# Projection pieces halved over more token turns, and two score rows placed ahead of the last turn, in a one-layer language model tower

## The chip, the cores and the metric

The kernel runs on one core of one Trainium2 chip. The metric is the device time of one execution in microseconds (us), the median of the runs. The engines are TensorE (PE: matmuls and transposes), VectorE (DVE), ScalarE (ACT), GpSimd (POOL) and SyncE (SP, here the issuer of most DMAs). They share memory and run their own instruction queues in order, tied together by semaphores.

## What is computed

2048 tokens (2 sequences of 1024) go through an embedding, one attention layer and one mixture-of-experts layer. In short:

```
is_hot  = hot_mask[tok]; hot_vec = hot_emb[tok2hot[tok]]; cold_vec = cold_emb[tok2cold[tok]] @ proj_w.T
h       = where(is_hot, hot_vec, cold_vec)                     # [2048, 512]
q, k, v = layernorm(h) @ w_project.T    (16 heads of 32)
h       = h + softmax(causal(q k^T / sqrt(32))) v @ w_out.T
h       = h + shared_ffn(layernorm(h)) + top-2 of 16 experts   # routed by layernorm(h) @ Wr.T + bias
```

tok2hot and tok2cold are counted out from the list of the 8000 hot ids in the kernel itself.

## The kernel before, in words

**Stages.** First a table over the vocabulary is built (64 pairs of one-hot products on PE). Then comes the token stage, on which the change acts, from about 35 us to 109 us of the span; then attention in 8 units (4 groups of heads by 2 sequences), the output projection, the router and the experts.

**Token stage.** The tokens are 16 tiles of 128 (NT = 16). A *look* (L1959 to L1967) is three bf16 matmuls that fetch a tile's table rows into one PSUM bank; a *lookup* (look_up, L1865) is the two reductions of DVE that read that bank. EARLY_LOOKS looks and lookups run ahead of the loop, the others inside it. row_numbers (L1877) turns the lookups of a group of tiles (ROWS_TO gives the group ends) into row numbers, and POOL gathers the cold and the hot rows of a tile with two indirect DMAs (L1764, L1768), tile by tile, with inv_std (L887) of an earlier tile behind each pair.

PE's loop runs over turns c = 0 to 18 (L1972). Turn c, in this order: transpose the cold rows of tile c (L1978), when its gather has landed; project tile c-1 (L1988), which needs ACT's copy of the transposed cold rows (L1805); transpose the normalized tile c-3 (L1996); look(EARLY_LOOKS + c - 1), while there are looks left; and a *piece* of unit 0's first projections if c is in FIRST_FILL (first_piece, L613). DVE's loop, iteration c: first_low for a piece (L594), embed(c) (L1890: L1895 adds the projected cold vector to the hot one, L1897 to L1899 are the statistics), norm(c-1) (L1901), a part of the weights' split (L537), look_up(EARLY_LOOKS + c - 1) and, at the end of a group, row_numbers. embed(c) needs the projection that PE issues in turn c+1. ACT's loop: copy of the cold transpose, copy of xnT for tile c-3 (L1809), first_high (L580).

**PSUM.** There are 8 banks. Before: cold transposes in banks 0 and 6 in turns, projections in 1 and 5, xn transposes in 2 and 3, looks in 4 and 5 (tiles 0 to 10) or 4 and 7 (tiles 11 to 15), pieces in 7. A look waits until the lookup two tiles back is done:

```
def look_bank(c):
    return bank(4 if c % 2 == 0 else 5 if c < EARLY_LOOKS else 7)
...
if c >= 2:
    pe.wait_ge(s_looked, 2 * (c - 1))
```

**First pieces.** FIRST_FILL = {7: 0, 8: 1, 10: 4, 12: 2, 14: 3, 16: 5} gives for a turn the piece: 0 and 1 are q and k for the first 512 tokens, 2 and 3 q and k for the next 512, 4 and 5 the values. A piece of q or k is 4 fp32 matmuls (8 records) of 512 columns; ACT writes its high part (first_high), DVE its low part (first_low), and both read the piece's bank.

**SP's queue.** It is in order (L1684): the store of tile c's h (L1686) when embed(c) is done; behind the store of tile 7 the 16 DMAs that stack q of the first half into q_stack and behind that of tile 8 the 16 for k_low (stack_half, L439 to L453), when the low part of the piece is ready; behind the store of tile 15 the 16 for the other half of q_stack and 16 for k_high. ACT and DVE begin attention when all 16 stores have landed.

**Attention.** A unit has 32 score rows of 128 queries (8 query tiles by 4 heads). Rows 0 to 15 need k_low and the first half of q_stack only; row 16 (NARROW) is the first that needs k_high (L690). Unit 0 begins with first_scores (L745), rows 0 and 1; row n+2 is issued in step n.

Of the kernel before, what the change touches and what calls it, by code (L numbers as in the profile page):

```python
# [11 lines left out]
F32 = mybir.dt.float32  # L12
# [8 lines left out]
P = 128  # L21
# [21 lines left out]
EARLY_LOOKS = 11  # L43
FIRST_FILL = {7: 0, 8: 1, 10: 4, 12: 2, 14: 3, 16: 5}
# [25 lines left out]
def build(nc, a, out):  # L70
    ctx = ExitStack()
    with ctx:
# [319 lines left out]
        ROWS_TO = [0, 2, 6, 11, NT]  # L392
# [81 lines left out]
        def look_bank(c):  # L474
            return bank(4 if c % 2 == 0 else 5 if c < EARLY_LOOKS else 7)

# [103 lines left out]
        def first_high(act, c):  # L580
# [6 lines left out]
            if side == 0:  # L587
                act.activation(part_hi[:, 0, cols], bank(7), ACT.Copy, scale=-ATT_SCALE).then_inc(s_hi, 1)
            elif side == 1:
                act.copy(part_hi[:, 1, cols], bank(7)).then_inc(s_hi, 1)  # L590
            elif half == 0:
                act.copy(v_unit[0][:, 0:4, :].rearrange("p a n -> p (a n)"), bank(7)).then_inc(s_fact, 1)

        def first_low(dve, c):  # L594
# [5 lines left out]
            if side < 2:  # L600
                dve.wait_ge(s_hi, HEAD + 2 * half + side + 1)
                if side == 0:
                    dve.scalar_tensor_tensor(out=part_lo[:, 0, cols], in0=bank(7), scalar=-ATT_SCALE,
                                             in1=part_hi[:, 0, cols].bitcast(F32), op0=ALU.mult,
                                             op1=ALU.subtract).then_inc(s_lo, 1)
                else:
                    dve.tensor_tensor(part_lo[:, 1, cols], bank(7), part_hi[:, 1, cols].bitcast(F32),
                                      ALU.subtract).then_inc(s_lo, 1)
            elif half == 1:
                dve.wait_ge(s_fill, HEAD + n + 1)  # L610
                dve.tensor_copy(v_unit[0][:, 4:8, :].rearrange("p a n -> p (a n)"), bank(7)).then_inc(s_fdve, 1)

        def first_piece(pe, c):  # L613

            f = FIRST_FILL[c]
            pe.wait_ge(s_wq if f < 4 else s_w, 16)
            pe.wait_ge(s_xC, 4 if f in (0, 1, 4) else 8)
            if f == 0:
                pe.wait_ge(s_looked, 2 * NT)
            elif f == 2:  # L620
                pe.wait_ge(s_fact, HEAD + 3)
            else:
                pe.wait_ge(s_lo, HEAD + {1: 1, 4: 2, 3: 3, 5: 4}[f])
            for k in range(KC):
                if f < 4:
                    side, half = f % 2, f // 2
                    mm = pe.matmul(bank(7), w_unit[:, k, side * P:(side + 1) * P],  # L627
                                   xnT[:, k, half * 512:half * 512 + 512],
                                   start=(k == 0), stop=(k == KC - 1), skip_group_check=True)
                else:  # L630
                    mm = value_products(pe, 0, f, k)
            mm.then_inc(s_fill, 1)

        def fill_piece(pe, u, b, f, k, loads):
# [17 lines left out]
            else:  # L652
                mm = value_products(pe, b, f, k)
# [3 lines left out]
        def value_products(pe, b, f, k):  # L657

            t0 = b * SEQ + ((f - 4) * 4 + k) * P
            for c in range(KC):  # L660
                mm = pe.matmul(bank(7)[:, k * P:(k + 1) * P], xnT[:, c, t0:t0 + P],  # L661
                               w_unit[:, c, 2 * P:3 * P], start=(c == 0), stop=(c == KC - 1))
            return mm

# [9 lines left out]
        def att_pe(pe):  # L674
# [78 lines left out]
            first_scores(0, 0, 0)  # L753
# [1301 lines left out]
```

## Time and profile before

| what | value |
|---|---|
| median of 3 runs | 965.74 us (964.69 to 966.0) |
| the profiled execution's own time | 964.48 us |
| its span in the trace | 962.7 us |
| PE busy | 899.1 us (93%) |
| DVE, ACT, POOL busy | 658.3, 604.0, 439.7 us |
| chain that ended last: PE, SP's queue, DVE, "issue" | 73%, 8%, 7%, 5% |

The busy times are sums over the whole span. The chain that ended last is followed back from the last instruction; a share of SP's queue in it means stretches in which the order and the pace of DMA issues set the end. The change touches only the stretch from about 35 to 128 us, so timelines of that stretch are what is to be read.

### The profile page before, as it was taken

How to read it: one execution, taken by the hardware profiler on the slowest of the kernel's cores; microseconds unless marked ns; L12 is line 12 of the kernel's file. 1: busy time of each engine (PE TensorE's matmuls, PEld its weight loads, DVE VectorE, ACT ScalarE, POOL GpSimd, SP SyncE). 2: the span in 40 equal slices, each digit the busy share in tenths (PEclk: the TensorE clock that was granted, in tenths of full speed). 3: DMA queues.
4: the chain of work that ended last, by engine and by line, in shares of the span. 5: the costliest groups of instructions: out<-in, count | busy, mean ns of one | idle time of the engine just before them, and what ended most of it. 6: DMA issues, size and time to landing. Idle time of an engine off the chain costs nothing.

```text
span 962.7 us, 21706 instructions
## 1 busy us (share of the span) xinstructions
PE 899.1 (93%) x6859; PEld 684.3 (71%) x6859; DVE 658.3 (68%) x1657; ACT 604.0 (63%) x1318; POOL 439.7 (46%) x486
## 2 busy tenths in 40 slices
PE   6778899999999999999997899999999999999995
PEld 5335678787887978878785677767776776776673
DVE  8886567576666757666675767868877666666662
ACT  6323577776777777777787833331157777777773
POOL 9276553533515346251500415633344577356332
PEclk9799999999999999999999999999999999999998
DMA  6135442324324242332313521271459478736530
GB/s 232 42 101 139 131 115 57 97 57 102 98 56 100 49 118 68 81 97 52 98 44 92 216 89 77 80 282 55 177 177 388 146 138 188 258 61 129 61 44 1
DMA packets 60514, 110.53 MB, mean 115 GB/s; under 512 B 15412, under 2 KB 21556, under 8 KB 58098
## 3 DMA queue, kind: packets, MB, share of 16 engines
q1 hardware_dynamic: 48082, 87.15, 29.1%
q0 software_dynamic: 12320, 21.99, 12.0%
q8 instruction: 57, 0.93, 0.4%
q14 instruction: 55, 0.45, 0.2%
HBM read 53.03 MB, written 25.17 MB: 81 GB/s over the span
## 4 chain that ended last, share of the span: by engine, by line
PE 73%; SPq 8%; DVE 7%; issue 5%; ACT 2%; POOL 2%; DMA 1%; ACTq 0%; POOLq 0%; DVEq 0%
PE psum L1576 13%; PE psum L705 10%; SPq L451 8%; PE psum L1654 8%; PE psum L718 6%; PE psum L695 6%; PE psum L661 5%; PE psum L648 5%; PE psum L670 5%; PE psum L1495 3%; PE psum L1608 2%; PE psum L1598 2%; PE psum L627 1%; PE psum L1587 1%; PE psum L721 1%
## 5 line engine op out<-in xcount | busy, mean ns | idle before, releaser
L792 ACT ACTIVATE probs<-psum,nmax 128x128 f32<-128x128 f32 (+7 forms) x256 | 191.2, 747 | 37.1 <-DVE nmax L834 33.7
L834 DVE CUSTOM_DVE_ANT_0 psum<-psum,mask_row 128x128 f32<-128x128 f32 (+7 forms) x256 | 192.1, 766 | 26.6 <-PE psum L695 25.1
L705 PE MATMUL psum<-ident,probs 128*128 128x128 f32 x1152 | 174.6, 276 | 13.0 <-ACT probs L792 6.1
L705 PEld LDWEIGHTS psum<-ident,probs 128*128 128x128 f32 x1152 | 134.1, 140 | 48.6 <-ACT probs L792 18.3
L777 ACT COPY probsT<-psum 128x512 f32<-128x512 f32 (+3 forms) x256 | 129.2, 505 | 33.2 <-PE psum L705 30.5
L1068 POOL DMA_INDIRECT out<-xnT,slot_out x47 | 81.4, 1732 | 100.8 <-DMA out<-xnT,slot_out 68.5
L488 POOL CAST part_hi<-full 128x512 fp32r<-128x512 f32 x28 | 17.1, 610 | 206.1 <-ACT full L565 160.3
L695 PE MATMUL psum<-k_low,q_stack 128*128 128x512 f32 (+2 forms) x256 | 104.3, 415 | 6.2 <-ACT probs L792 2.6
L849 DVE TENSOR_TENSOR attnT<-psum,z_rows 128x128 f32<-128x128 f32 x64 | 18.6, 291 | 111.3 <-ACT z_rows L799 111.3
L1654 PE MATMUL psum<-w_dn,gated_T 128*128 x188 | 88.4, 593 | 1.0 <-ACT gated_T L1131 1.0
L1418 DVE TENSOR_TENSOR w_lo<-w_gu,w_hi 128x1024 fp32r<-128x1024 f32 x48 | 58.7, 1225 | 40.4 <-ACT w_hi L1160 39.4
L1418 DVE TENSOR_TENSOR ws_lo<-w_gu,ws_hi 128x1024 fp32r<-128x1024 f32 x46 | 56.3, 1226 | 37.5 <-ACT ws_hi L1160 36.7
L718 PE MATMUL psum<-probsT,v_unit 128*32 128x128 f32 x2304 | 76.2, 275 | 0.0
L515 POOL TENSOR_TENSOR x_lo<-xnT,x_hi 128x512 fp32r<-128x512 f32 x56 | 71.8, 1282 | 4.4
L718 PEld LDWEIGHTS psum<-probsT,v_unit 128*32 128x32 f32 x2304 | 59.0, 109 | 15.5 <-ACT probsT L777 7.8
L661 PE MATMUL psum<-w_unit,xnT 128*128 128x128 f32 x512 | 66.6, 275 | 0.0
L779 DVE COPY probsT<-psum 128x128 f32<-128x128 f32 (+3 forms) x128 | 62.2, 486 | 3.9 <-PE psum L705 2.9
L695 PEld LDWEIGHTS psum<-k_low,q_stack 128*128 128x128 f32 x256 | 51.2, 203 | 15.0 <-ACT probs L792 10.9
L661 PEld LDWEIGHTS psum<-w_unit,xnT 128*128 128x128 f32 x512 | 61.7, 192 | 0.0
L1145 ACT ACTIVATE xnT<-psum,slot_w 128x512 f32<-128x512 f32 x47 | 32.4, 689 | 41.7 <-PE psum L1654 41.7
L1160 ACT CAST w_hi<-w_gu 128x1024 fp32r x48 | 50.3, 1050 | 8.9 <-issue 5.6
L1654 PEld LDWEIGHTS psum<-w_dn,gated_T 128*128 128x128 f32 x188 | 35.5, 189 | 27.6 <-issue 23.7
(280 smaller groups left out, 2134.2 us busy)
## 6 DMA issues: line engine op xcount, KB each, us to landing
w_gu<-in_wgu SPq DMA_DIRECT2D x16, 1024.0 KB, 6.7
q_stack<-part_hi SPq DMA_DIRECT2D x128, 64.0 KB, 2.0
q_stack<-part_lo SPq DMA_DIRECT2D x128, 64.0 KB, 2.0
w_dn<-in_wd SPq DMA_DIRECT2D x16, 512.0 KB, 8.6
out<-acc SPq DMA_DIRECT2D x17, 256.0 KB, 3.6
hot_all<-xn SPq DMA_DIRECT2D x4, 1024.0 KB, 8.6
h_scratch<-hot_all SPq DMA_DIRECT2D x16, 256.0 KB
k_low<-part_hi SPq DMA_DIRECT2D x64, 64.0 KB, 2.0
```

The lines of the kernel that those rows point to most:

```text
L451: sp.dma_start(dst.bitcast(F32), src[32 * h:32 * h + 32, side, half * 512:half * 512 + 512].bitcast(F32)).then_inc((s_high if half else s_ ...
L661: mm = pe.matmul(bank(7)[:, k * P:(k + 1) * P], xnT[:, c, t0:t0 + P], w_unit[:, c, 2 * P:3 * P], start=(c == 0), stop=(c == KC - 1))
L695: mm = pe.matmul(dst[:, c0:c1], qs, ks[:, h, 0:c1 - c0], start=True, stop=True)
L705: mm = pe.transpose(bank(4 + m % 2)[:, (j - 4 * k) * P:(j - 4 * k + 1) * P], probs[n % PSLOTS][:, j * P:(j + 1) * P], ident[:, :])
L718: pe.matmul(bank(6)[32 * h:32 * h + 32, 0:P], v_unit[b][:, j, 32 * h:32 * h + 32], probsT[i % 2][:, h, j * P:(j + 1) * P], start=(j == 0), ...
L777: eng.copy(dst, src).then_inc(s_Ca, 1)
L792: act.activation(probs[n % PSLOTS][:, 0:(i + 1) * P], score_bank(n)[:, 0:(i + 1) * P], ACT.Exp, bias=nmax[:, n % 4:n % 4 + 1], scale=-1.0, ...
L834: dve.tensor_tensor_reduce(out=row, in0=row, in1=mask_row[:, (QT - 1 - i) * P:QT * P], scale=1.0, scalar=3.0e38, op0=ALU.add, op1=ALU.min, ...
L1068: pool.indirect_dma_start(out=out, out_offset=bass.IndirectOffsetOnAxis(ap=slot_out[:, j:j + 1], axis=0), in_=y_rows[j % ROUTED_RING], in_ ...
L1418: dve.tensor_tensor(w_lo[j % 2][:, k, :].rearrange("p k n -> p (k n)"), w_gu[:, bass.ds(slot, 1), k, :].rearrange("p o k n -> p (o k n)"), ...
L1576: mm = pe.matmul(bank(2 + p), x[:, p, k * P:(k + 1) * P], w[p][:, k, :], start=(k == 0 and t == 0), stop=(k == KC - 1 and t == 2), skip_gr ...
L1654: mm = pe.matmul(bank(6 + p), gated_T[:, p, k * P:(k + 1) * P], w_dn[:, bass.ds(half, 1), k, :].rearrange("p o n -> p (o n)"), start=(k == 0),
```

## The change

- The first pieces are halved: each half (2 of the 4 k-steps) goes into one of the turns 6 to 17 (FIRST_TURN = 6), the second half in the turn that FIRST_FILL names. Pieces use banks 7 and 6 in turns.
- The cold transposes move into two parts of bank 0, and each waits for the copy of the one before.
- Looks: eight run ahead of the loop (EARLY_LOOKS = 8). From tile 8 on all use bank 4, and each waits for the lookup of the tile before.
- The row numbers come in five groups, ending at tiles 2, 6, 10, 13 and 16.
- DVE's first_low stands behind norm in its iteration.
- The first two score rows of unit 0 (scores_ahead) are issued in turn 17, ahead of the transposes of tile 15 in turn 18. What first_scores waited for is waited for at attention's start.

```diff
-EARLY_LOOKS = 11
-FIRST_FILL = {7: 0, 8: 1, 10: 4, 12: 2, 14: 3, 16: 5}
+EARLY_LOOKS = 8
+FIRST_FILL = {7: 0, 9: 1, 11: 4, 13: 2, 15: 3, 17: 5}
+FIRST_TURN = 6
...
-        ROWS_TO = [0, 2, 6, 11, NT]
+        ROWS_TO = [0, 2, 6, 10, 13, NT]
...
         def look_bank(c):
-            return bank(4 if c % 2 == 0 else 5 if c < EARLY_LOOKS else 7)
+            return bank(5 if c % 2 and c < EARLY_LOOKS else 4)
+
+        def first_bank(f):
+            return bank(7 - list(FIRST_FILL.values()).index(f) % 2)
...
-            f = FIRST_FILL[c]
-            pe.wait_ge(s_wq if f < 4 else s_w, 16)
-            pe.wait_ge(s_xC, 4 if f in (0, 1, 4) else 8)
-            if f == 0:
-                pe.wait_ge(s_looked, 2 * NT)
-            elif f == 2:
-                pe.wait_ge(s_fact, HEAD + 3)
-            else:
-                pe.wait_ge(s_lo, HEAD + {1: 1, 4: 2, 3: 3, 5: 4}[f])
-            for k in range(KC):
+            half_piece = (c - FIRST_TURN) % 2
+            f = FIRST_FILL[c + 1 - half_piece]
+            if half_piece == 0:
+                pe.wait_ge(s_wq if f < 4 else s_w, 16)
+                pe.wait_ge(s_xC, 4 if f in (0, 1, 4) else 8)
+                if f == 3:
+                    pe.wait_ge(s_fact, HEAD + 3)
+                elif f in (4, 2, 5):
+                    pe.wait_ge(s_lo, HEAD + {4: 1, 2: 2, 5: 3}[f])
+                elif f == 1:
+                    pe.wait_ge(s_coldC, c)
+            for k in range(2 * half_piece, 2 * half_piece + 2):
...
-            mm.then_inc(s_fill, 1)
+            if half_piece:
+                mm.then_inc(s_fill, 1)
...
+        def scores_ahead(pe):
+
+            pe.wait_ge(s_low[0], STACKED)
+            pe.wait_ge(s_coldC, NT)
+            pe.wait_ge(s_h, NT - 1)
+            for h in range(2):
+                pe.matmul(bank(h)[:, 0:256], q_stack[:, h, 0:P], k_low[0][:, h, 0:256], start=True,
+                          stop=True).then_inc(s_S, 1)
...
-            first_scores(0, 0, 0)
+            pe.wait_ge(s_fact, HEAD + 3)
+            pe.wait_ge(s_fdve, HEAD + 3)
             unit(0, 0, 0, False, True)
...
-                    act.copy(cold_T[:, c % 2, :], bank(6 if c % 2 else 0)[:, 0:P]).then_inc(s_coldC, 1)
+                    act.copy(cold_T[:, c % 2, :], bank(0)[:, c % 2 * P:c % 2 * P + P]).then_inc(s_coldC, 1)
...
             for c in range(NT + 1):
-                if c in FIRST_FILL and c < NT:
-                    first_low(dve, c)
                 if c < NT:
                     embed(c)
                 if c >= 1:
                     norm(c - 1)
+                if c in FIRST_FILL:
+                    first_low(dve, c)
...
-            first_low(dve, NT)
+            first_low(dve, NT + 1)
...
             def look(c):
                 if c >= 2:
-                    pe.wait_ge(s_looked, 2 * (c - 1))
+                    pe.wait_ge(s_looked, 2 * (c if c >= EARLY_LOOKS else c - 1))
...
-                    if c >= 2:
-                        pe.wait_ge(s_coldC, c - 1)
-                    pe.transpose(bank(6 if c % 2 else 0)[:, 0:P], cold_lat[c][:, :],
+                    if c >= 1:
+                        pe.wait_ge(s_coldC, c)
+                    pe.transpose(bank(0)[:, c % 2 * P:c % 2 * P + P], cold_lat[c][:, :],
                                  ident[:, :]).then_inc(s_coldT, 1)
...
-                if c in FIRST_FILL:
+                if FIRST_TURN <= c < FIRST_TURN + 2 * FILLS:
                     first_piece(pe, c)
+                if c == NT + 1:
+                    scores_ahead(pe)
             pe.wait_ge(s_xC, NT)
+            pe.wait_ge(s_lo, HEAD + 4)
             att_pe(pe)
```

## Rows read from the trace of the kernel before

**Rows 1.** Chain of work, 36 to 130 us: start us, us, what

```profile
62.34 3.81 DMA cold_all<-in_cold_emb,cold_row
...
103.69 0.32 SPq L1686
...
125.61 2.03 DMA k_high<-part_lo
```

**Rows 2.** Timeline of PE, 88 to 128 us: start us, us, instructions, [idle before, releaser]

```profile
88.20 3.60 PE L627 MATMUL psum<-xnT,w_unit 128*128 128x512 f32 x8
91.64 0.27 PE L1978 MATMUL psum<-ident,cold_all 128*128 128x128 f32 x1
91.75 1.02 PE L1988 MATMUL psum<-projT,cold_T 128*128 128x512 f32 x2
92.61 0.60 PE L1996 MATMUL psum<-ident,xn 128*128 128x128 f32 x4
...
95.42 0.66 PE L1996 MATMUL psum<-ident,xn 128*128 128x128 f32 x4 [1.24 <-DVE xn L1906]
...
109.00 0.74 PE L695 MATMUL psum<-k_low,q_stack 128*128 128x256 f32 x4 [0.78 <-ACT xnT L1809]
...
127.78 0.47 PE L695 MATMUL psum<-k_low,q_stack 128*128 128x512 f32 x1 [0.42 <-DMA k_high<-part_lo]
```

**Rows 3.** Timeline of SP's queue, 73 to 107 us

```profile
73.69 2.53 SPq L451 DMA_DIRECT2D q_stack<-part_hi  x4
...
94.56 9.45 SPq L1686 DMA_DIRECT2D h_scratch<-hot_all  x7
104.05 2.41 SPq L451 DMA_DIRECT2D q_stack<-part_hi  x4
```

**Rows 4.** Timeline of DVE, 50 to 103 us

```profile
50.02 0.69 DVE L1895 TENSOR_TENSOR hot_all<-hot_all,psum 128x512 f32<-128x512 f32 x1 [0.42 <-PE psum L1988]
...
52.30 0.69 DVE L1895 TENSOR_TENSOR hot_all<-hot_all,psum 128x512 f32<-128x512 f32 x1 [0.45 <-PE psum L1988]
...
55.29 0.68 DVE L1895 TENSOR_TENSOR hot_all<-hot_all,psum 128x512 f32<-128x512 f32 x1
...
58.28 0.08 DVE L1873 DVE_READ_ACCUMULATOR prod<-iota_bf,tok_lo,psum 128x1 f32 x1
58.28 0.68 DVE L1895 TENSOR_TENSOR hot_all<-hot_all,psum 128x512 f32<-128x512 f32 x1
...
77.78 0.68 DVE L1895 TENSOR_TENSOR hot_all<-hot_all,psum 128x512 f32<-128x512 f32 x1
...
92.47 0.69 DVE L603 SCALAR_TENSOR_TENSOR part_lo<-psum,part_hi 128x512 fp32r<-128x512 f32 x1 [1.94 <-ACT part_hi L588]
...
102.98 0.68 DVE L1895 TENSOR_TENSOR hot_all<-hot_all,psum 128x512 f32<-128x512 f32 x1
```

**Rows 5.** Timeline of PE, 47 to 60 us

```profile
47.91 2.07 PE L1988 MATMUL psum<-projT,cold_T 128*128 128x512 f32 x2
...
52.09 0.38 PE L1964 MATMUL psum<-tab_a,tok_ohT 125*128 125x512 bf16 x1
...
52.59 1.02 PE L1988 MATMUL psum<-projT,cold_T 128*128 128x512 f32 x2
...
59.84 0.33 PE L1978 MATMUL psum<-ident,cold_all 128*128 128x128 f32 x1 [0.93 <-DMA cold_all<-in_cold_emb,cold_row]
```

**Rows 6.** Timeline of POOL: the gather of tile 2's cold rows

```profile
45.40 1.00 POOL L1764 DMA_INDIRECT cold_all<-in_cold_emb,cold_row  x1 [0.30 <-issue]
```

**Rows 7.** Stretches of 2 us: length, busy us of PE, PEld, DVE, ACT, POOL, PEclk, DMA share, GB/s

```profile
34.00:36.00 2.00, 0.97 (x4) 0.46 (x5) 0.94 (x6) 0.00 (x0) 0.00 (x0) 0.67 1.02 336
...
50.00:52.00 2.00, 2.00 (x6) 0.95 (x5) 1.72 (x4) 0.27 (x1) 0.37 (x2) 0.57 0.36 106
...
58.00:60.00 2.00, 0.98 (x7) 0.45 (x6) 1.90 (x6) 0.59 (x1) 1.80 (x3) 1.00 0.40 67
```

More of the change, by code:

```diff
@@ L587, in first_high @@
             if side == 0:
-                act.activation(part_hi[:, 0, cols], bank(7), ACT.Copy, scale=-ATT_SCALE).then_inc(s_hi, 1)
+                act.activation(part_hi[:, 0, cols], first_bank(f), ACT.Copy, scale=-ATT_SCALE).then_inc(s_hi, 1)
             elif side == 1:
-                act.copy(part_hi[:, 1, cols], bank(7)).then_inc(s_hi, 1)
+                act.copy(part_hi[:, 1, cols], first_bank(f)).then_inc(s_hi, 1)
             elif half == 0:
-                act.copy(v_unit[0][:, 0:4, :].rearrange("p a n -> p (a n)"), bank(7)).then_inc(s_fact, 1)
+                act.copy(v_unit[0][:, 0:4, :].rearrange("p a n -> p (a n)"), first_bank(f)).then_inc(s_fact, 1)
         def first_low(dve, c):
@@ L602, in first_low @@
                 if side == 0:
-                    dve.scalar_tensor_tensor(out=part_lo[:, 0, cols], in0=bank(7), scalar=-ATT_SCALE,
+                    dve.scalar_tensor_tensor(out=part_lo[:, 0, cols], in0=first_bank(f), scalar=-ATT_SCALE,
                                              in1=part_hi[:, 0, cols].bitcast(F32), op0=ALU.mult,
@@ L606, in first_low @@
                 else:
-                    dve.tensor_tensor(part_lo[:, 1, cols], bank(7), part_hi[:, 1, cols].bitcast(F32),
+                    dve.tensor_tensor(part_lo[:, 1, cols], first_bank(f), part_hi[:, 1, cols].bitcast(F32),
                                       ALU.subtract).then_inc(s_lo, 1)
@@ L610, in first_low @@
                 dve.wait_ge(s_fill, HEAD + n + 1)
[L611 removed]
+                dve.tensor_copy(v_unit[0][:, 4:8, :].rearrange("p a n -> p (a n)"), first_bank(f)).then_inc(s_fdve, 1)
         def first_piece(pe, c):
[L615 to L624 removed]
+            half_piece = (c - FIRST_TURN) % 2
[10 more added lines that the diff above has]
+            for k in range(2 * half_piece, 2 * half_piece + 2):
                 if f < 4:
                     side, half = f % 2, f // 2
[L627 removed]
+                    mm = pe.matmul(first_bank(f), w_unit[:, k, side * P:(side + 1) * P],
                                    xnT[:, k, half * 512:half * 512 + 512],
@@ L652, in fill_piece, with value_products @@
             else:
-                mm = value_products(pe, b, f, k)
+                mm = value_products(pe, b, f, k, bank(7))
             if k == KC - 1:
                 mm.then_inc(s_fill, 1)
-        def value_products(pe, b, f, k):
+        def value_products(pe, b, f, k, dst):
             t0 = b * SEQ + ((f - 4) * 4 + k) * P
             for c in range(KC):
-                mm = pe.matmul(bank(7)[:, k * P:(k + 1) * P], xnT[:, c, t0:t0 + P],
+                mm = pe.matmul(dst[:, k * P:(k + 1) * P], xnT[:, c, t0:t0 + P],
                                w_unit[:, c, 2 * P:3 * P], start=(c == 0), stop=(c == KC - 1))
             return mm
+        def scores_ahead(pe):
[5 more added lines that the diff above has]
+                          stop=True).then_inc(s_S, 1)
         def output_tile(pe, c):
```

2 lines of the change are left out of this document (1 added, 1 removed).

## The prediction

> **What bounds the kernel now.** I read the page first (PE is busy 93% of the span, so a stretch in which PE waits is worth looking for), then the chain of work over the stretch that the change touches, then the timelines of the engines on it, last POOL and the clock. "Tile c" is a tile of 128 tokens, "turn c" PE's turn c, "iteration c" DVE's; embed(c) is the L1895 addition.
>
> The chain runs back from score row 16 of unit 0, the first that needs the high halves of the keys: it starts at 127.78 after a wait of 0.42 us for k_high, whose last copy lands at 127.64 (125.61 + 2.03) [rows 1, 2]. Those copies stand in SP's queue: 32 stacking DMAs from 104.05, and just ahead of them the store of tile 15 at 103.69, which waits for embed(15) at 102.98 [rows 1, 3, 4]. Attention's first product starts at 109.00, but it ends at this same gate. So the end of the kernel moves with embed(15), as long as PE reaches row 16 in time; it took 18.8 us from 109.00 to 127.78.
>
> What sets embed(15)? In the piece turns PE works 3.43 us on a piece (88.20 to 91.64), DVE can't start embed until its low part has come out of that piece, and PE then idles 1.24 us for the norm (95.42) [rows 2]. Two turns take 7.7 us. Before that, in turns 4 to 7, PE waits for the gather of the cold rows (0.93 us at 59.84) [rows 5], and DVE is just as full: embed to embed 2.99 us (55.29 to 58.28) with a lookup in each iteration [rows 4].
>
> **The change, part by part.**
>
> Halved pieces and banks 6 and 7 in turns. The products are the same 6 pieces; 12 halves of 1.73 us (3.45 / 2). A turn without a piece costs PE 0.11 + 0.86 + 0.44 = 1.41 us (91.64, 91.75, 92.61, and 0.44 to the next transpose) [rows 2], with a half piece 3.14. The low part moves behind norm on DVE and the next half goes to another bank, so the idle 1.24 per pair should go: turns 9 to 16 run at 3.14 each instead of a mean of 3.60 (embed(8) at 77.78 to embed(15) at 102.98, seven turns, 25.2 us) [rows 4]. Gain in these seven: 25.2 - 22.0 = 3.2 us. I give back 0.5 for iteration 8, where DVE has lookup 15 and a group of row numbers to do and norm(8) comes late for turn 11.
>
> Eight looks ahead of the loop instead of eleven. Three looks and one group of row numbers leave the stretch before turn 0. But tile 2's cold rows are issued only at 45.40, and a gather lands 3.8 us after (62.34 + 3.81) [rows 1, 6]: 49.2. Turn 2 waits for it, and its projection takes 2.11 us at the clock of then (47.91 to embed at 50.02) [rows 4, 5], so embed(1) comes at about 51.8, against 52.30. Gain: 0.5.
>
> The looks left over. This is the term that decides. From tile 8 on all looks use bank 4, and look(c) waits for 2c reductions: for lookup(c-1). In turn t PE issues the projection of tile t-1, then look(t+7), and that waits for lookup(t+6). DVE does lookup(t+6) in iteration t-1, behind embed(t-1), which needs the projection that PE has just issued in the same turn; embed(t) needs the projection of turn t+1, queued on PE behind the look. So no part of DVE's iteration lies beside PE's turn any more. Before, the wait was for a look two back, with banks 4 and 7, and hid. The new period is: embed's start to lookup's end 3.07 (55.29 to 58.28 + 0.08) [rows 4]; handover 0.05 (47.91 + 2.07 to 50.02 shows 0.04) [rows 4, 5]; look and transpose 0.50 (52.09 to 52.59); projection 1.02 and handover 0.04 [rows 5]. Sum 4.68 us a turn, against 3.1 before. It holds for looks 9 to 15, turns 2 to 8. In turns 6, 7 and 8 the half piece stands behind the look, also in line: 4.68 + 1.73 = 6.41; in iteration 7 DVE has the first low part, 0.69 (92.47), between norm and lookup [rows 4].
>
> Clock. The periods above are at the granted clock 1.00. It was 1.00, then fell to half near 34.7 (a mean of 0.67 in 34 to 36), where PE was busy less than half of the time, and rose again within 50 to 52 (mean 0.57), in which PE is busy throughout [rows 7]. In the new kernel PE is busy from about 46.9 to 51.7 (projection 0, look 8, projection 1), as it was before the rise; I take it that the clock rises there again. The other end is that it stays at 1.2 GHz: then look and transpose cost twice 0.50 and the projection 2.11, 6.23 a turn, 1.55 more.
>
> The Trainium skill, "TensorE: Matmul & The Clock Gate", Part 1 (The HAM clock gate), says of this that "the default state is throttled, and activity releases the throttle": with PE idle for some 2.7 us of every 4.7, it speaks against this change, and by it the sum could be the one with the 1.55 in each turn. The trace agrees so far as it shows the fall after idleness and the rise after work.
>
> Gathers. The row numbers now come in iterations 2, 5 and 8. The last group is ready about 95, the gather of tile 13 lands near 99, and turn 13 is at about 103; covered by 4 us. If that cover went, each us late would be a us.
>
> Cold transposes share bank 0 and wait for the copy of the tile before; PE waited for that same copy one instruction later, so nothing. The wait of the first half piece for xnT of tile 3: about 0.7 us beside the look's stall of turn 6 (look(13) is later than that copy), nothing. ACT: same work, at other turns; nothing behind it is waited for.
>
> Scores ahead. Two products of row 0 move ahead of the last turn and could save at most the 0.78 of waiting at 109.00 [rows 2]. Row 16 waits for k_high anyway, so I count 0; at least one such wait stands ahead of it. At the other end, had SP time to spare, it would be worth 0.8.
>
> SP. Its queue is passed in order. The first q_stack copies wait for low part 0 (73.69 before), then 20.9 us of stacking and a store (73.69 to 94.56) stand ahead of tiles 9 to 15's stores [rows 3]. Now low part 0 comes after norm in iteration 7: 83.3, 2.2 (an iteration of 2.99 without its lookup) and 0.7 make 86.2, low part 1 in iteration 9, about 97.5, k_low's stack (half of the 20.9) ends near 108, six stores of 0.63 (2.53 / 4) end at 112. embed(15) is later than that, by a little.
>
> **Sum.** embed(1) 51.8; turns 3 to 6 bring embed(2) to embed(5), 4 x 4.68 = 18.7: 70.5; embed(6) and embed(7) 2 x 6.41 = 12.8: 83.3; embed(8) 6.41 + 0.69 = 7.1: 90.4 (before 77.78: 12.6 later). Then 22.0 + 0.5: embed(15) at 112.9, before 102.98. So +9.9 us. SP starts the high stacks that much later, k_high lands 23.6 later as before, near 137.5. PE, 18.8 us from attention's start (109.0 + 9.9), is there at the same time. Everything behind is shifted. Profiled execution: 964.48 (span 962.7) + 9.9 = 974.4; the median of the runs, 965.74, is 1.26 above it, so the forecast is 965.74 + 9.9 = 975.6. One measurement of this kernel can't tell under 0.2% (1.9 us) from nothing.
>
> **Rivals.**
>
> *The clock stays low* until the half pieces of turn 6: four turns at +1.55, 6.2 us more, 981.8. For: PE idles over half of each of these turns. Against: before, in 58 to 60, PE was busy for 0.98 of 2 us and the clock stayed at 1.00 [rows 7]. The Trainium skill's rule above is this case. Chance 0.28.
>
> *Faster.* The place is look(t+7) in turns 2 to 8. If lookup(t+6) were over when PE gets there, that is, if DVE ran one tile ahead of PE's projection, the stall wouldn't exist and only the better part would be left. Then low part 0 comes about 75.2 (behind embed and norm of its iteration instead of ahead of them, so 1.5 later than where its copies start now, 73.69), SP is through 20.9 us of stacking and seven stores of 0.63 at about 100.7 instead of 104.05: -3.3, 962.4. It decides at zero slack between the end of lookup and PE's arrival; by the order of both queues there is none. Chance 0.09.
>
> *Half paid.* The look is late in only some turns, for example because DVE's iteration gets shorter by itself: 2 to 6 us slower, 968 to 972. Chance 0.08. *Nothing to be seen*, gain and loss cancel: 0.03.
>
> **How the numbers follow.** Forecast 0.52. Slower: 0.52 + 0.28 + 0.08 = 0.88; faster 0.09; same 0.03. The range takes the forecast with its uncertain ends (1.26 of which execution, 0.5 of DVE, SP's close finish) and the low clock, with 1 us over: 970 to 983. Left out are the faster case, the same and part of the half paid one.
>
> **What would show it.** PE idle before L1964 for DVE prod, some 2.4 us in each of turns 2 to 8; embeds 4.7 apart, then 6.4, and 3.1 from tile 9 on; embed(15) near 113, k_high near 137.5 and row 16 right behind it. The granted clock from 52 to 75 tells the rival. Wrong it is if L1964 waits under 1 us, or if row 16 no longer waits for k_high.

## The result and the profile after

| what | before | after |
|---|---|---|
| median of 4 runs of each on one chip | 965.87 us (964.69 to 968.79) | 982.84 us (979.93 to 984.92) |
| ratio to before | | 1.0169 (95%: 1.013 to 1.0208) |
| the profiled execution's own time | 964.48 us | 984.63 us |
| its span | 962.7 us | 982.8 us |
| mean granted clock of PE over the span | 0.988 | 0.971 |
| embed(1), embed(8), embed(15) start at | 52.30, 77.78, 102.98 | 50.95, 99.93, 122.78 |
| first k_high row (row 16) starts at | 127.78 | 147.09 |

The changed kernel is 17.0 us slower, where 9.9 were forecast; the median is just inside the range (970 to 983), but not by the case that was taken as likeliest, and two of its four executions (984.63 and 984.92) lie outside. The executions lie 5 us apart, and they go with the mean granted clock: 979.93 us at 0.978, 981.05 at 0.976, the two longest at 0.971 and 0.973. The profiled one is near the upper end. It is 20.15 us over the profiled execution of before; all reckoning below is between these two, so what it gives for the clock is the price in one of the longer executions.

Line numbers have moved: embed is L1912 (L1895 before), the lookup L1890, the look L1981 to L1983 (L1964), the cold transpose L1995, the projection L2005, the transpose of xn L2013, a piece L633, the scores ahead L678, score rows L711, SP's stores L1703.

**Which wait grew.** The waits of PE between 44 and 126 us in the changed kernel (engine and line, what it waited for: us in total, times, longest us):

```profile
PE psum L1981 <- DVE prod L1890: 19.0, 7, 3.4
PE psum L1995 <- DMA cold_all<-in_cold_emb,cold_row: 1.9, 1, 1.9
PE psum L2013 <- DVE xn L1923: 0.7, 2, 0.5
```

and the same view of the kernel before, between 44 and 110 us:

```profile
PE psum L1996 <- DVE xn L1906: 5.8, 5, 1.3
PE psum L1978 <- DMA cold_all<-in_cold_emb,cold_row: 4.3, 4, 1.7
PE psum L1964 <- DVE prod L1873: 1.6, 2, 1.3
```

The waits for the norm (5.8 us) and for gathers (4.3 us) shrink, as the change means them to. The wait of the look for DVE's lookup goes from 1.6 us to 19.0 us, in seven times, the seven looks 9 to 15.

**The embeds.** The stage goes by them. The timeline of DVE in the changed kernel (start us, us, instruction, [idle before, releaser]) at embed(1), (2), (5), (6), (8) and (15):

```profile
50.95 0.69 DVE L1912 TENSOR_TENSOR hot_all<-hot_all,psum 128x512 f32<-128x512 f32 x1 [1.01 <-PE psum L2005]
...
56.97 0.69 DVE L1912 TENSOR_TENSOR hot_all<-hot_all,psum 128x512 f32<-128x512 f32 x1 [2.95 <-PE psum L2005]
...
74.90 0.69 DVE L1912 TENSOR_TENSOR hot_all<-hot_all,psum 128x512 f32<-128x512 f32 x1 [2.77 <-PE psum L2005]
...
83.08 0.69 DVE L1912 TENSOR_TENSOR hot_all<-hot_all,psum 128x512 f32<-128x512 f32 x1 [3.64 <-PE psum L2005]
...
99.93 0.69 DVE L1912 TENSOR_TENSOR hot_all<-hot_all,psum 128x512 f32<-128x512 f32 x1 [5.09 <-PE psum L2005]
...
122.78 0.69 DVE L1912 TENSOR_TENSOR hot_all<-hot_all,psum 128x512 f32<-128x512 f32 x1 [0.72 <-PE psum L2005]
```

From embed(1) to embed(5) they are 6.02, 6.02, 6.04 and 5.87 us apart, then 8.18, 8.07 and 8.78, where 4.68, 6.41, 6.41 and 7.10 were forecast. From embed(8) to embed(15) it is 22.85 us: 3.26 a turn, 25.20 before [rows 4]. So the sum against before is -1.35 (embed(1) at 50.95, not 52.30), +23.5 from there to embed(8) (48.98 us, not 25.48), and -2.35 for the last seven: +19.8.

**One stalled turn.** The timeline of PE in the changed kernel shows a whole period, from one look to the next, and the work just before it:

```profile
49.00 1.92 PE L2005 MATMUL psum<-projT,cold_T 128*128 128x512 f32 x2
54.09 0.61 PE L1981 MATMUL psum<-tab_a,tok_ohT 125*128 125x512 bf16 x1 [3.17 <-DVE prod L1890]
...
55.02 1.91 PE L2005 MATMUL psum<-projT,cold_T 128*128 128x512 f32 x2
56.73 1.06 PE L2013 MATMUL psum<-ident,xn 128*128 128x128 f32 x4
60.11 0.61 PE L1981 MATMUL psum<-tab_a,tok_ohT 125*128 125x512 bf16 x1 [2.32 <-DVE prod L1890]
```

The projection at 55.02 ends at 56.93, embed starts at 56.97, the lookup that follows it on DVE ends at 60.05 (59.97 + 0.08, beside the 3.07 us of the prediction), and the look starts at 60.11. Nothing lies beside anything: 2.84 us of PE, 0.04, 3.08 us of DVE, 0.06. That is the serial turn of the prediction. But look and transpose take 0.93 us (54.09 to 55.02), not 0.50, and the projection 1.91, not 1.02.

**The clock.** Stretches of 2 us of the changed kernel (length, busy us of PE, PEld, DVE, ACT, POOL, then the granted clock, share of the DMA engines, GB/s):

```profile
50.00:52.00 2.00, 0.92 (x2) 0.00 (x0) 1.01 (x2) 0.00 (x0) 1.80 (x3) 0.50 0.49 159
...
54.00:56.00 2.00, 1.92 (x6) 1.06 (x7) 0.03 (x2) 0.27 (x1) 1.56 (x2) 0.50 0.14 21
...
58.00:60.00 2.00, 0.00 (x0) 0.00 (x0) 1.93 (x8) 0.41 (x1) 0.79 (x1) 0.50 0.35 131
...
70.00:72.00 2.00, 0.00 (x0) 0.00 (x0) 1.93 (x7) 0.12 (x1) 0.88 (x2) 1.00 0.35 131
72.00:74.00 2.00, 1.81 (x6) 1.12 (x7) 0.13 (x2) 0.27 (x1) 1.70 (x2) 0.60 0.15 17
```

Before, the mean over 50 to 52 was 0.57, with PE busy throughout, and it was 1.00 afterwards [rows 7]. Here PE works only for the first 0.92 us of that stretch and then stands for 3.17 us. The clock stays at half of its rate (1.2 GHz) until about 69. After that it is badly timed as well as low: it is at 2.4 GHz in 70 to 72, in which PE does nothing, and 0.60 in the next stretch, in which PE works; the same again in 84 to 86 (1.00, PE idle) and 86 to 88 (0.51, PE busy 1.76 us). Not every working stretch is so slow: 78 to 80 has 0.81 and 82 to 84 has 0.84. The slices of the page that show the token stage (the granted clock in tenths, 40 slices of the span) say the same more coarsely, `57` here for `99` before in the third and fourth slice:

```profile
PEclk9757999999999999999999999999999999999998
```

**The end of the stage.** The timeline of SP's queue in the changed kernel:

```profile
94.08 2.53 SPq L452 DMA_DIRECT2D q_stack<-part_hi  x4
...
118.54 5.27 SPq L1703 DMA_DIRECT2D h_scratch<-hot_all  x7
123.86 2.42 SPq L452 DMA_DIRECT2D q_stack<-part_hi  x4
```

and the timeline of PE around attention's start and at row 16:

```profile
127.33 0.48 PE L678 MATMUL psum<-k_low,q_stack 128*128 128x256 f32 x2
...
128.98 0.50 PE L711 MATMUL psum<-k_low,q_stack 128*128 128x256 f32 x2 [0.73 <-ACT xnT L1826]
...
147.09 0.47 PE L711 MATMUL psum<-k_low,q_stack 128*128 128x512 f32 x1 [0.86 <-DMA k_high<-part_lo]
```

The seven stores of tiles 9 to 15 take 5.27 us here, 9.45 before [rows 3]: SP comes close to being late, but the last store still waits for embed(15) at 122.78. The last stacks (the second half of q_stack, then k_high) start 19.8 us later than before, k_high's last copy lands at 146.95 (144.92 + 2.03 in the chain of work), and row 16 starts right behind it, 19.3 us later. From row 16 to the end of the span it is 835.7 us (982.8 - 147.09), 834.9 before.

### The profile page after: what moved, and what is told of

It is laid out like the page before. It is cut to its first block, busy times and chain, and to the rows that moved or that the text cites. A ratio compares the mean times of both kernels' runs of the same rounds, so it can differ in the third digit from the quotient of the medians.

```text
span 982.8 us, 21715 instructions
## 1 busy us (share of the span) xinstructions
PE 910.7 (93%) x6859; PEld 689.8 (70%) x6859; DVE 659.3 (67%) x1664; ACT 604.4 (61%) x1318; POOL 439.9 (45%) x486
## 4 chain that ended last, share of the span: by engine, by line
PE 76%; DVE 9%; SPq 6%; issue 4%; ACT 2%; DMA 1%; POOL 0%; ACTq 0%; DVEq 0%; POOLq 0%
PE psum L1593 13%; PE psum L721 11%; PE psum L1671 8%; PE psum L734 6%; SPq L452 6%; PE psum L711 6%; PE psum L655 6%; PE psum L668 5%; PE psum L686 4%; PE psum L1512 3%; PE psum L1625 2%; PE psum L2005 2%; PE psum L1615 2%; PE psum L633 2%; PE psum L737 1%
## 5 line engine op out<-in xcount | busy, mean ns | idle before, releaser
L851 DVE CUSTOM_DVE_ANT_0 psum<-psum,mask_row 128x128 f32<-128x128 f32 (+7 forms) x256 | 192.0, 766 | 24.8 <-PE psum L711 23.6
L1085 POOL DMA_INDIRECT out<-xnT,slot_out x47 | 79.1, 1682 | 102.2 <-DMA out<-xnT,slot_out 65.0
L711 PE MATMUL psum<-k_low,q_stack 128*128 128x512 f32 (+2 forms) x254 | 104.0, 416 | 5.8 <-ACT probs L809 2.6
L711 PEld LDWEIGHTS psum<-k_low,q_stack 128*128 128x128 f32 x254 | 50.9, 203 | 14.5 <-ACT probs L809 9.9
```

The lines of the kernel that those rows point to most:

```text
L711: mm = pe.matmul(dst[:, c0:c1], qs, ks[:, h, 0:c1 - c0], start=True, stop=True)
L851: dve.tensor_tensor_reduce(out=row, in0=row, in1=mask_row[:, (QT - 1 - i) * P:QT * P], scale=1.0, scalar=3.0e38, op0=ALU.add, op1=ALU.min, ...
L1085: pool.indirect_dma_start(out=out, out_offset=bass.IndirectOffsetOnAxis(ap=slot_out[:, j:j + 1], axis=0), in_=y_rows[j % ROUTED_RING], in_ ...
```

## The experiments

The theory: the look that waits for the lookup just before it makes the turn serial, and with the clock, which the stall itself keeps low, that is the whole loss. The rivals: the loss comes from elsewhere in the change (the halved pieces, cold transposes in one bank, the scores ahead), or from the single bank as such. The kernel before was run anew with each set: 964.53 us (first set), 965.29 (second), 966.03 (third).

**The change without its looks.** Eleven early looks, two banks for the looks and the old wait come back; everything else of the change stays. The pieces go to banks 6 and 7 from the other end, so that bank 7 is free when the first one comes.

```diff
-EARLY_LOOKS = 8
+EARLY_LOOKS = 11
-        ROWS_TO = [0, 2, 6, 10, 13, NT]
+        ROWS_TO = [0, 2, 6, 11, NT]
...
-            return bank(5 if c % 2 and c < EARLY_LOOKS else 4)
+            return bank(4 if c % 2 == 0 else 5 if c < EARLY_LOOKS else 7)
...
-            return bank(7 - list(FIRST_FILL.values()).index(f) % 2)
+            return bank(6 + list(FIRST_FILL.values()).index(f) % 2)
...
-                    pe.wait_ge(s_coldC, c)
+                    pe.wait_ge(s_looked, 2 * NT)
...
-                    pe.wait_ge(s_looked, 2 * (c if c >= EARLY_LOOKS else c - 1))
+                    pe.wait_ge(s_looked, 2 * (c - 1))
```

> The changed kernel with the looks put back: eleven ahead of the loop, the other five in turns 1 to 5 in banks 4 and 7 in turns, each waiting for the lookup two back; the row number groups of before; piece halves, scores ahead and all else as changed, the pieces in banks 6 and 7 with piece 0 in bank 6. Theory (the wait for the lookup just before is the whole loss): no idle of over 1 us before a look in the loop; embeds 3.1 apart from tile 8 on; embed(15) near 97 instead of 102.98 before and 122.8 changed; k_high lands near 123.6, bound now by SP's queue from about 75 on; some 4 us faster than the kernel before, about 962. PE waits 2 to 3 us for k_high at row 16. Rival (the halved pieces or the shared cold bank cost too): embed(15) above 103 and the time above that of the kernel before.

Measured: 961.4 us (960.01 to 964.04, 10 runs), a ratio of 0.9971 (0.996 to 0.9981). It is 0.3% faster than the kernel before, and 21.4 us faster than the changed kernel's 982.84 (of another set). PE's waits between 44 and 128 us:

```profile
PE psum L711 <- DMA k_high<-part_lo: 2.6, 1, 2.6
...
PE psum L1981 <- DVE prod L1890: 1.6, 2, 1.3
```

and SP's queue, in which the stack of the first q starts at 74.17 and that of the second at 100.17:

```profile
74.17 2.53 SPq L452 DMA_DIRECT2D q_stack<-part_hi  x4
...
96.07 4.05 SPq L1703 DMA_DIRECT2D h_scratch<-hot_all  x7
100.17 2.58 SPq L452 DMA_DIRECT2D q_stack<-part_hi  x4
```

The look waits 1.6 us again, as before, and embed(15) comes at 96.48, which is 6.5 us earlier than before. Yet only 3.1 us are gained, since SP isn't through with its stacks: its seven stores take 4.05 us, 0.58 each, so none of them waits, and the last stack starts 3.9 us earlier (104.05 before) [rows 3]. So the halved pieces, the shared bank of the cold transposes and the scores ahead are together a gain, no loss, and the rivals "elsewhere in the change" fall. The number of early looks, their banks, their wait and the groups of row numbers went back together here; the next experiment takes the wait by itself.

**The wait alone, in the kernel before.** One line: banks, early looks and pieces stay as they were.

```diff
-                    pe.wait_ge(s_looked, 2 * (c - 1))
+                    pe.wait_ge(s_looked, 2 * (c if c >= EARLY_LOOKS else c - 1))
```

> The kernel before with one edit: the looks of the loop (tiles 11 to 15, turns 1 to 5) wait for the lookup just before instead of two back; banks, pieces and all else as before. Theory: four turns (2 to 5) get the serial chain; at 4.7 us each (clock 1.00) embed(15) moves by 7 us, about 973; at 6.0 each (clock half) by 11 to 12, about 977. Since the looks are over before the pieces begin, turns 6 to 8 pay nothing. Rival (one bank more or less does not matter, the pieces in line with the looks are the cost): under 3 us.

Measured: 975.69 us (971.43 to 977.31, 4 runs), a ratio of 1.01 (1.0072 to 1.0127): 11.2 us over the kernel before, for one wait of five looks. PE's waits between 44 and 122 us (two of the six, 1.6 us in total, stand ahead of the loop as before; the other four are 2.3 to 3.3 us each):

```profile
PE psum L1964 <- DVE prod L1873: 12.0, 6, 3.3
```

The embeds of tiles 1, 2 and 5 on DVE's timeline:

```profile
51.69 0.69 DVE L1895 TENSOR_TENSOR hot_all<-hot_all,psum 128x512 f32<-128x512 f32 x1
...
57.70 0.69 DVE L1895 TENSOR_TENSOR hot_all<-hot_all,psum 128x512 f32<-128x512 f32 x1 [2.94 <-PE psum L1988]
...
75.30 0.69 DVE L1895 TENSOR_TENSOR hot_all<-hot_all,psum 128x512 f32<-128x512 f32 x1 [2.94 <-PE psum L1988]
```

and the clock:

```profile
52.00:54.00 2.00, 0.00 (x0) 0.00 (x0) 1.90 (x6) 0.00 (x0) 1.51 (x3) 0.95 0.44 165
54.00:56.00 2.00, 1.18 (x5) 0.84 (x6) 0.76 (x4) 0.00 (x1) 1.79 (x3) 0.50 0.28 40
...
122.00:124.00 2.00, 2.00 (x8) 1.66 (x7) 1.24 (x6) 1.21 (x7) 0.35 (x1) 0.52 0.43 107
```

Four turns took 23.6 us, 5.9 each, and embed(15) comes at 113.86, 10.9 late. The two banks are still there, so the bank as such isn't what costs: the order is. Here the clock had already risen, at about 50.4, and it fell again at about 53.8, within the first stall of 3.25 us. Of its four executions the fastest, 971.43 us, has a mean granted clock of 0.985, the profiled one 0.974: the same order of work costs 7 us or 13, and the difference goes with the clock. Both cases of the expectation, 973 and 977, so have their executions.

The last line above is from the start of attention in the same trace. PE had waited 0.78 and then 0.75 us there, and the clock fell to half at about 122, for some 3.5 us; in the kernel before PE waits the same 0.78 (at 109.00) and 0.75 us there, and the clock stayed at 1.00:

```profile
119.88 0.73 PE L695 MATMUL psum<-k_low,q_stack 128*128 128x256 f32 x4 [0.78 <-ACT xnT L1809]
121.37 0.33 PE L705 MATMUL psum<-ident,probs 128*128 128x128 f32 x1 [0.75 <-ACT probs L792]
```

So the length of one wait doesn't settle by itself whether the clock falls.

**The stall filled with work.** The changed kernel, with nine matmuls whose result nobody reads (into bank 6, free until the second piece comes), ahead of the wait of each of the looks 9 to 15: 63 matmuls more, same waits.

```diff
+                if c > EARLY_LOOKS:
+                    for _ in range(9):
+                        pe.matmul(bank(6), tok_ohT[:, 0, :], tab_a[:, :], start=True, stop=True,
+                                  skip_group_check=True)
                 if c >= 2:
                     pe.wait_ge(s_looked, 2 * (c if c >= EARLY_LOOKS else c - 1))
```

> The changed kernel, with nine extra bf16 matmuls of 512 columns into the unused bank 6 ahead of the wait of each look of turns 2 to 8 (their result is read by nobody). They fill the 2.3 to 3.4 us in which PE waits. Theory (half of the loss is the clock, which falls because PE idles there): granted clock 1.00 from turn 3 or 4 on; embeds 4.7 apart in turns 4 to 6, 6.4 in 6 to 8; embed(15) near 113; about 8 to 9 us faster than the changed kernel, 973 to 976, though PE does more work. Rival (the wait alone is the cost, the clock no part of it): no faster than the changed kernel's 982.8, or slower by the work added.

Measured: 975.37 us (975.21 to 977.36, 4 runs), a ratio of 1.0118 (1.01 to 1.0136). With more work for PE the kernel is 7.5 us faster than the changed one. The embeds of tiles 5, 8 and 15 on DVE's timeline, the projection and the added matmuls on PE's, and the clock:

```profile
69.53 0.69 DVE L1912 TENSOR_TENSOR hot_all<-hot_all,psum 128x512 f32<-128x512 f32 x1 [1.63 <-PE psum L2009]
...
89.59 0.69 DVE L1912 TENSOR_TENSOR hot_all<-hot_all,psum 128x512 f32<-128x512 f32 x1 [3.39 <-PE psum L2009]
...
112.45 0.69 DVE L1912 TENSOR_TENSOR hot_all<-hot_all,psum 128x512 f32<-128x512 f32 x1 [0.71 <-PE psum L2009]
```

```profile
49.04 1.58 PE L2009 MATMUL psum<-projT,cold_T 128*128 128x512 f32 x2
50.46 2.11 PE L1979 MATMUL psum<-tab_a,tok_ohT 125*128 125x512 bf16 x9
...
55.60 2.11 PE L1979 MATMUL psum<-tab_a,tok_ohT 125*128 125x512 bf16 x9
58.50 0.39 PE L1985 MATMUL psum<-tab_a,tok_ohT 125*128 125x512 bf16 x1 [0.79 <-DVE prod L1890]
```

```profile
54.00:56.00 2.00, 2.00 (x12) 1.23 (x11) 0.63 (x1) 0.46 (x2) 1.52 (x3) 1.00 0.09 10
```

embed(1) is at 50.66, and the next are 4.71, 4.70, 4.73, 4.73, 6.49, 6.48 and 7.09 us apart. This is the forecast's turn by turn (4.68, 6.41, 6.41, 7.10), at the clock that it took. The wait of the look is 0.79 us in the turn shown and the filler about 2: together the idle time that the serial order leaves at 2.4 GHz. So the loss splits: from embed(1) to embed(8) it is 25.48 us before, 38.93 here, 48.98 in the changed kernel. In the profiled executions the order of the work costs 13.45 us, the clock 10.05; between the medians the clock is 7.5.

When the clock rises is another matter. Here it rose at about 50.2, still in the projection at 49.04 and ahead of the first added matmul at 50.46, behind the same work that in the changed kernel went on to 50.91 without a rise. So the filler didn't raise it. But with the filler it stayed: from 52 to 104 every stretch of 2 us is at 1.00.

**No scores ahead.** The changed kernel with the first two score rows where they were before.

```diff
+            first_scores(0, 0, 0)
-            pe.wait_ge(s_fact, HEAD + 3)
-            pe.wait_ge(s_fdve, HEAD + 3)
             unit(0, 0, 0, False, True)
...
-                if c == NT + 1:
-                    scores_ahead(pe)
```

> The changed kernel with the first two score rows back at attention's start. Theory: row 16 waits for k_high and SP's queue sets that, so nothing: within 1 us of the changed kernel (its own executions lie 5 us apart), with attention's first products some 0.5 us later and a shorter wait before row 16. Rival: slower by the 0.8 us that the rows had saved.

Measured: 983.13 us (976.24 to 984.71, 4 runs), a ratio of 1.0168 (1.0126 to 1.021), the same as with them within the spread; the second q stack starts at 123.83 (123.86 with them). In the changed kernel the scores ahead are worth nothing in the traces, since the stacks of SP set row 16 either way. The runs are too far apart to tell half a us. One of the four, 976.24 us, has a mean granted clock of 0.984 where the profiled one has 0.969: by that mean an execution of the serial order in which most of the clock's price wasn't paid, near the 975.6 of the forecast. It has no trace.

**What holds the good part back.** In the kernel of the first experiment SP is the end: 32 stacking copies and the stores pass its queue one after the other. Two edits start from it. The first has the low part of piece 0 ahead of embed(7) again, as before the change, so that SP's first stack starts earlier; the second takes 8 of the 32 first copies from SP and lets ACT issue them, two in each of the turns 11 to 14.

```diff
             for c in range(NT + 1):
                 if c < NT:
+                    if c == 7:
+                        first_low(dve, c)
                     embed(c)
...
-                if c in FIRST_FILL:
+                if c in FIRST_FILL and c != 7:
                     first_low(dve, c)
```

> The kernel of two look banks (e1) with one edit: the low part of piece 0 stands ahead of embed(7) on DVE again, so that SP's first stacking copies can go as soon as the store of tile 7 is out. Theory (from there to row 16 SP's queue is full and sets the end): first q_stack copy near 72.6 instead of 74.17, k_high 1.5 us earlier, row 16 near 121.6, some 1 to 1.5 us faster than e1; PE's later start of embed(7) costs nothing at the end. Rival (after e1 PE or DVE sets the end again): no change from e1.

```diff
-            for r in range(4):
+            for r in range(2 if u == 0 and side == 1 and half == 0 else 4):
...
+        def stack_by_act(act, i):
+            if i == 0:
+                act.wait_ge(s_lo, HEAD + 2)
+            for n in (2 * i, 2 * i + 1):
+                r, h = 2 + n // GH, n % GH
+                act.dma_start(k_low[0][32 * r:32 * r + 32, h, :].bitcast(F32),
+                              part_lo[32 * h:32 * h + 32, 1, 0:512].bitcast(F32)).then_inc(s_low[0], 16)
...
+                if 11 <= c < 15:
+                    stack_by_act(act, c - 11)
```

> The kernel of two look banks (e1) with 8 of the 16 DMAs that stack k_low (its low parts) issued by ACT, two in each of its turns 11 to 14, instead of by SP. Theory: SP's queue is 5 us shorter ahead of the stores, then waits for embed(15); the high stacks start near 97.8 instead of 100.17, k_high lands near 120.7, row 16 follows at 121.1 with a wait under 0.5 us instead of 2.56, and the granted clock stays at 1.00 there instead of falling to half over 122.7 to 129. 2 us for the gate and up to 2.5 for the clock: 957 to 959.5. Rival (the clock's fall at row 16 is no cost, or ACT's issues delay PE by as much): within 1 us of e1.

Both edits in one kernel, and the first experiment again, beside them on the same chip:

> The edits of e5 and e6 together on e1. Theory: with SP relieved by e6 the gate is embed(15) and PE, so e5's edit adds nothing more: within 0.7 us of e6. Rival: both gains add, 1 us or more below e6.

> The kernel of e1 once more, as the partner of e5 to e7 on the same chip. Expected: 960 to 964 as in e1, some 3 us below the kernel before; PE waits some 2.5 us before row 16 and the clock falls there in a part of its executions.

Measured, with 965.29 for the kernel before:

| kernel | us (range, runs) | ratio (95%) | row 16 at | its wait |
|---|---|---|---|---|
| looks as before, again | 961.41 (960.93 to 963.89, 5) | 0.996 (0.9947 to 0.9973) | 124.29 | 2.91 |
| low part first | 958.23 (956.62 to 962.94, 6) | 0.994 (0.9918 to 0.9961) | 121.17 | 1.35 |
| stack by ACT | 957.13 (956.99 to 959.02, 5) | 0.992 (0.9906 to 0.9934) | 121.05 | 0.70 |
| both | 957.63 (957.08 to 960.37, 5) | 0.9921 (0.9908 to 0.9934) | 121.04 | 0.78 |

The gain of the two edits is the same and doesn't add up: both shorten the same queue. In the kernels with ACT's copies the last of the seven stores waits for embed(15) again (they take 7.54 and 8.82 us), the last stacks start some 1.1 us behind it, and row 16 still waits for k_high: embed(15) sets the end through SP's queue, and PE is there only 0.70 to 0.78 us early. Row 16 in the first experiment's kernel, and the clock around it:

```profile
123.14 0.77 PE L711 MATMUL psum<-k_low,q_stack 128*128 128x512 f32 x1 [2.56 <-DMA k_high<-part_lo]
```

```profile
120.00:122.00 2.00, 0.58 (x13) 0.19 (x5) 0.29 (x1) 0.71 (x3) 0.39 (x1) 1.00 0.41 100
124.00:126.00 2.00, 2.00 (x8) 1.76 (x7) 1.15 (x4) 0.99 (x2) 0.00 (x0) 0.50 0.94 284
128.00:130.00 2.00, 2.00 (x10) 1.86 (x9) 1.18 (x3) 1.88 (x5) 1.05 (x1) 0.66 0.43 106
```

and in the one with ACT's copies:

```profile
121.05 0.46 PE L720 MATMUL psum<-k_low,q_stack 128*128 128x512 f32 x1 [0.70 <-DMA k_high<-part_lo]
```

```profile
122.00:124.00 2.00, 2.00 (x13) 1.57 (x12) 1.66 (x6) 1.89 (x5) 0.00 (x0) 1.00 0.93 284
```

Here is more than the wait. Where PE stood 2.56 us (and 2.91 in the second trace of that kernel) its clock fell to half within the wait, at about 122.5 (123.9 in the second), though PE had worked at full rate for long before. With the waits of 1.35, 0.78 and 0.70 us at this place it stayed. From row 16 to the seventh k_low product behind it, it is 14.26 and 13.02 us in the two traces with the fall and 11.89 us in the other three, as in the kernel before: 2.4 and 1.1 us. The rest of the span can't show this price: behind row 16 it is 838.1 and 837.8 us with the fall, but also 837.6 in the kernel with both edits, without it.

The low part first is 3.2 us faster than its pair. Against the pair's trace its first stack starts 1.96 us earlier (72.55, 74.51), the last stacks 2.74 (98.18, 100.92), and row 16 comes 3.1 us earlier. So the queue gave more than the 1.5 us expected; how much of the 3.2 is the clock, the runs don't separate.

**With a shorter queue, do the scores ahead count?** The ACT kernel without them, the ACT edit alone in the kernel before, and the ACT kernel again, with 966.03 for the kernel before:

> The kernel of e6 with the first two score rows back at attention's start. In e6 row 16 waits only 0.70 us for k_high, so PE's own way to it counts almost. Theory: attention's start and row 15 come about 0.7 us later, the wait before row 16 goes to near nothing, row 16 moves by 0 to 0.3: the same as e6 within 0.5 us. Rival: slower than e6 by the whole 0.7 or more.

> The kernel before with e6's edit alone: 8 of k_low's 16 stacking DMAs issued by ACT. Theory: there SP waits for embed(15) anyway (seven stores in 9.45 us), so the relief of SP buys at most nothing: within 1 us of the kernel before, and the gain of e6 belongs to the halved pieces, which the relief lets through. Rival: the relief is the gain by itself, 3 us or more faster than the kernel before.

> The kernel of e6 once more, as the partner of the other two on the same chip: 957 to 958.5, 7 to 8 us below the kernel before.

| kernel | us (range, runs) | ratio (95%) | embed(15) | row 16 at | its wait |
|---|---|---|---|---|---|
| ACT kernel, no scores ahead | 959.66 (957.67 to 963.52, 6) | 0.9927 (0.9907 to 0.9947) | 97.41 | 123.08 | none |
| kernel before, stack by ACT | 965.52 (963.65 to 967.13, 12) | 0.9993 (0.9982 to 1.0004) | 103.15 | 127.37 | none |
| ACT kernel again | 961.3 (958.5 to 961.8, 6) | 0.9937 (0.9921 to 0.9952) | 98.90 | 123.00 | 0.63 |

The ACT edit alone gives nothing in the kernel before. SP's queue there shows why:

```profile
89.67 14.51 SPq L1695 DMA_DIRECT2D h_scratch<-hot_all  x7
104.22 2.41 SPq L451 DMA_DIRECT2D q_stack<-part_hi  x4
```

The seven stores take 14.51 us because the last waits for embed(15); the time that ACT saves SP is spent waiting. SP's 8 copies are worth something only after the projection turns have become shorter. Without the scores ahead PE reaches row 16 with no wait, 25.7 us behind embed(15), and with them 24.2 (121.05 less 96.89) and 24.1: by these traces, one execution each, they are worth some 1.5 us once SP's queue is short, where at most 0.3 was expected. The medians (959.66 and 961.3, with intervals that overlap) don't show it, so this stays open.

The ACT kernel itself was expected at 957 to 958.5 in this set and came at 961.3. Its trace has a hole of its own. The timeline of ACT:

```profile
86.60 0.59 ACT L605 COPY v_unit<-psum 128x512 f32<-128x512 f32 x1 [3.29 <-remote]
```

ACT stands for 3.29 us ahead of the copy of the values' piece, and the embed of tile 11 is 2.7 us later than in the first trace of this kernel (86.68, 83.95). What held it isn't shown by any row, and the median of that set (961.3, against 957.13 in the set before) may carry it or not. Against the kernel before, the ratios of the two sets are 0.9937 and 0.992.

## Why the prediction was right in direction and short in size

**The serial look: right.** The forecast said that look(t+7) waits for a lookup behind an embed that waits for PE's own projection, in turns 2 to 8. The trace shows seven waits there, and the first experiment shows that without them the change is a gain. The serial order was priced at 4.68, 6.41, 6.41 and 7.10 us a turn; with PE kept busy the chip gives 4.72, 6.49, 6.48 and 7.09, and a median of 975.37 us where 975.6 were forecast. That the total fits so closely is in part luck: embed(1) came 1.1 us early, and behind row 16 it took 1.5 us more than before.

**The clock: the term that was short.** The prediction had it: "In the new kernel PE is busy from about 46.9 to 51.7 (projection 0, look 8, projection 1), as it was before the rise; I take it that the clock rises there again." PE was busy from 45.90 to 50.9, and the clock didn't rise; 3.17 us of waiting came instead. The step read the rise of before off the work ahead of it and took it for lasting. Both parts fail. The rise doesn't come at a fixed point of the work: it came at about 51.7 before, at 50.4 and 50.2 in the traces of the second and the third experiment, and not at all by 50.91 here. And where it came and the stall followed, it was lost: in the one-line experiment the first stall of 3.25 us took it back. The forecast's evidence against the low clock, 0.98 us of work in 58 to 60 at 1.00, was one stretch out of turns of about 3 us, with idle times such as the 0.93 us at 59.84 [rows 5]; the changed kernel idles 2.3 to 3.4 us at a time. The term was put at nothing; it measured 10.05 us between the profiled executions and 7.5 between the medians.

By the Trainium skill, "TensorE: Matmul & The Clock Gate", Part 1 (The HAM clock gate), the engine is slow by default and activity releases it. The trace agrees: 0.50 while PE worked 3.7 us in each 6.0, and 1.00 in 54 to 56 with the filler in the same turns. The prediction cited that sentence against its own case and gave the case 0.28. In the executions of the serial order on record the low clock is the common case, but not the only one (976.24 and 971.43 us are at 0.984 and 0.985).

**The low clock's own size: wrong too.** That rival was four turns at 1.55 us more, 6.2, and 981.8. Four turns cost 5.23 more (6.02 where 6.23 was forecast: look and transpose 0.93, not 1.00, the projection 1.91, not 2.11). But the rival ended it at turn 6, at the half pieces, as work that would bring the clock back. The clock was back for a first time at 69, ahead of any half piece, and from there on it was high mostly at times at which PE stood: turns 6 to 8 took 25.03 us, where 19.92 were forecast, 5.1 more. Together 10.3, less the 0.85 by which embed(1) came early, plus 0.35 behind embed(8): embed(15) at 122.78, 9.9 after the forecast's 112.9. So the rival's 981.8 lies near the median of 982.84 by luck: its price for the clock was 6.2.

**The other terms.** embed(1) was due at 51.8 by the gather of tile 2 and came at 50.95. The turns from 9 on were forecast at 3.14, plus 0.5 in one; 22.85 us were measured for 22.5, of which the first took 4.46 (4.47 with the stall filled and the clock at 1.00) and the others 3.07 on average: the 0.5 given back for iteration 8 was too little by 0.8, and the 3.14 a little too much. The gathers for turns 11 and later stayed covered; no wait for them shows behind turn 1. SP's queue: the forecast had it through its stores just ahead of embed(15), and with embed(8) and embed(15) both some 10 us later than forecast, it was (5.27 us for seven stores, the last waiting). The scores ahead were counted 0, and the experiment without them shows no difference that the spread would let through. The 23.6 us from SP's start of the last stacks to the landing of k_high held: 23.1 (123.86 to 146.95). Of the span's 20.1 us, 19.3 are there at row 16, and 0.8 lie behind it. In the changed kernel the clock falls once more there (0.74 in 640 to 645, 0.92 in 645 to 650), in the kernel before it doesn't; whether that is the 0.8, no run shows.

**The faster rival.** It gave 962.4 for the case that the look weren't stalled, with the last stack at 100.7. The first experiment is nearly that case (eleven early looks, not eight): 961.4, and 100.17. The rival lacked the wait of 2.56 us at row 16 and the fall of the clock there.

## What to carry to other kernels

When a wait is moved one step nearer in a loop of two engines, write out the round trip: here one line made turns of about 3.1 us serial (4.7 us, and 5.9 at the clock that followed) and cost 11 us by itself. Price such a stall twice, once as idle time and once as the clock at which everything around it then runs, and give the second price a range: executions of one kernel lay 5 to 8.5 us apart, in step with their mean clock. When a queue in order (SP's) and an engine finish close together, a gain on one alone shows little: the shorter turns brought 3 to 4 us until 8 copies left the queue (then 8.2 and 4.7 in two sets), and the 8 copies nothing until the turns were short.

## What the runs showed of the hardware

- The clock can come at the wrong times. From 70 us on the changed kernel had 1.00 in stretches in which PE did nothing and 0.50 to 0.84 in most of those in which it worked; a loop that alternates 2.3 to 3.4 us of waiting with 3.7 to some 5 us of work had most of its work done at half rate, over some 40 us.
- One wait can be enough: in the one of 2.56 us at row 16 the clock went from 1.00 to 0.50 (0.66 still in 128 to 130), which cost 2.4 us more than the wait itself, and in one of 2.91 us 1.1 us more. In a wait of 1.35 us at the same place it stayed. But no length of a wait can be called safe from this: behind waits of 0.78 and 0.75 us it fell to 0.50 in one kernel's trace and stayed at 1.00 in another's.
- The same kernel gets a different clock from execution to execution: the changed one without the scores ahead ran from 984.62 us at a mean of 0.969 to 976.24 us at 0.984.
- Work that nobody needs made the kernel faster: 63 matmuls added, 7.5 us less.
